# Two of 25 neighbour rows taken from SBUF by 0/1 products on TensorE, in a two-layer graph kernel

## The reference

```python
h = jnp.maximum(_layernorm(x, axis=-1), 0.0)
# layer 0, A = adj, S = 25
scores = jnp.where(A != 0, -jnp.arange(N), neg_inf)
vals, idx = jax.lax.top_k(scores, S)
feats = jax.vmap(lambda x, i: x[i])(h, idx)
feats = jnp.where((vals > neg_inf)[..., None], feats, neg_inf)
agg = feats.max(axis=2)
agg = jnp.where((degree <= S)[..., None], jnp.maximum(agg, 0.0), agg)
x = x + relu(concat([h, agg], -1) @ W0 + b0)
# layer 1
h = jnp.maximum(_layernorm(x, axis=-1), 0.0)
hidden = h @ W1.T
attn = leaky_relu(a1[:, :, None] + a2[:, None, :], 0.2)
attn = softmax(jnp.where(adj > 0, attn, attn - 1e12), -1)
x = x + attn @ hidden + bias
```

## Time and profile before

| what | us |
|---|---|
| median of 3 runs (4226.17 to 4229.52) | 4229.43 |
| the profiled execution, time | 4228.84 |
| the profiled execution, span | 4226.7 |
| GpSimd busy | 3064.6 (73%) |
| VectorE busy | 2596.7 (61%) |
| TensorE busy, products | 2441.5 (58%) |
| ScalarE busy | 1565.1 (37%) |
| mean granted clock of TensorE, share of full | 0.756 |

### The profile page before, as it was taken

One profiled execution on the slowest core, in us unless ns is written; L12 is line 12 of the kernel. 1 busy time (PEld: TensorE's weight loads), 2 busy tenths in 40 slices (PEclk: granted clock), 3 DMA queues, 4 the chain that ended last, 5 costly groups with the idle time before them and its releaser, 6 DMA issues. The chain is left out here.

```text
span 4226.7 us, 34008 instructions
## 1 busy us (share of the span) xinstructions
PE 2441.5 (58%) x8788; PEld 1510.5 (36%) x8788; DVE 2596.7 (61%) x6764; ACT 1565.1 (37%) x1748; POOL 3064.6 (73%) x3204
## 2 busy tenths in 40 slices
PE   1213345656555656565666565566556566656898
PEld 0111123433333434333334333343333343434565
DVE  5654566666666666666665676566676666566653
ACT  3112233334343434343434433334433334434354
POOL 4777777777777777777777777777777777777740
PEclk6555567777777878777878777777777777777899
DMA  7455568777777777777777777777777776777530
GB/s 288 150 189 174 189 180 232 195 219 214 230 211 228 204 223 216 217 220 219 212 215 216 216 228 211 228 207 209 218 228 215 224 207 213 214 211 223 179 106 35
DMA packets 477367, 867.56 MB, mean 205 GB/s; under 512 B 308298, under 2 KB 309204, under 8 KB 456660
## 3 DMA queue, kind: packets, MB, share of 16 engines
q0 software_dynamic: 153600, 419.64, 36.0%
q1 hardware_dynamic: 305140, 378.64, 28.8%
q10 hardware_dynamic: 18432, 67.12, 4.2%
HBM read 690.98 MB, written 119.54 MB: 192 GB/s over the span
## 5 line engine op out<-in xcount | busy, mean ns | idle before, releaser
L560 POOL DMA_INDIRECT near<-table_dram,idx x3200 | 3064.4, 958 | 1011.4 <-issue 961.1
L1406 PE MATMUL acc<-hid,wgt 128*128 128x257 f32 x4096 | 1051.5, 404 | 61.6 <-ACT wgt L642 54.4
L964 DVE TENSOR_TENSOR highest<-near,highest 128x512 f32<-128x512 f32 x1280 | 890.4, 696 | 43.8
L1406 PEld LDWEIGHTS acc<-hid,wgt 128*128 128x128 f32 x4096 | 817.0, 203 | 199.1 <-ACT wgt L642 72.2
L961 DVE TENSOR_TENSOR highest<-near 128x512 f32<-128x512 f32 x128 | 89.7, 701 | 814.8 <-DMA near<-table_dram,idx 813.4
L606 ACT ACTIVATE nm_t<-adj_i,big_c 128x2048 bf16<-128x2048 int32 x128 | 501.5, 3944 | 7.0 <-DMA adj_i<-in_adj_dram 3.4
L636 ACT ACTIVATE pen<-a_b,a_rise 128x512 f32<-128x512 f32 x432 | 296.5, 690 | 427.0 <-DMA nm_c<-nm_q 397.9
L1339 PE MATMUL bank<-w_sb,h_t 128*128 128x256 f32 x1024 | 348.0, 499 | 134.4 <-ACT h_t L739 134.4
L642 ACT ACTIVATE wgt<-pen,a_slope 128x512 f32<-128x512 f32 x448 | 304.2, 679 | 292.4 <-PE pen L1399 254.6
L739 ACT ACTIVATE h_t<-bank 128x512 f32<-128x512 f32 x128 | 76.0, 594 | 849.3 <-PE bank L1331 849.3
L898 DVE MAX8 top<-key 128x8 f32<-128x256 f32 (+1 forms) x1024 | 351.4, 384 | 5.6
(11 more groups left out here) (161 smaller groups left out, 2355.4 us busy)
## 6 DMA issues: line engine op xcount, KB each, us to landing
adj_i<-in_adj_dram SPq DMA_DIRECT2D x128, 1024.0 KB
nmask_dram<-nm_t ACTq DMA_DIRECT2D x128, 512.0 KB
nm_q<-nmask_dram SPq DMA_DIRECT2D x28, 2048.0 KB, 8.7
near<-table_dram,idx POOLq DMA_INDIRECT x3200
h_q<-table_dram SPq DMA_DIRECT2D x32, 512.0 KB, 3.9
x_q<-in_x_dram SPq DMA_DIRECT2D x32, 512.0 KB, 5.4
xmid_dram<-x_q SPq DMA_DIRECT2D x32, 512.0 KB, 4.3
o_q<-xmid_dram SPq DMA_DIRECT2D x32, 512.0 KB, 8.0
```

The source lines that it names most:

```text
L560: pool.indirect_dma_start(out=near[:, t % 2, k, :], out_offset=None, in_=table, in_offset=bass.IndirectOffsetOnAxis(ap=idx[:, t, k:k + 1], ...
L964: nc.vector.tensor_tensor(highest[:, :], pair(k), highest[:, :], ALU.max).then_inc(mx_step, 1)
L1406: mm = nc.tensor.matmul(acc[:, t, 0:C + 1], wgt_part(j)[:, t * P:(t + 1) * P], hid[:, bass.ds(batch * NJ + j, 1), 0:C + 1].rearrange("p a ...
```

## The change

In steps 0 to 29, tiles 1, 2 and 3, GpSimd gathers 23 rows instead of 25. The last two come from SBUF: a new tile `tab` holds all 2048 rows of the batch (`NJ` = 16 blocks of 128), loaded every fourth step in place of `h_q`. ScalarE widens the two index columns to 128x256, TensorE transposes them so that every partition holds all 128 indices, and ScalarE copies them back and clears `highest`. VectorE then compares, for each of the 16 blocks, the indices with that block's row numbers, into one of four buffers that lie over `bits` and `key2`; TensorE multiplies each 0/1 matrix, once for each of the two rows, with the block in `tab` and accumulates into `highest`. `maximum` starts from that. GpSimd's descriptor scratch is cut from its default to 8192 bytes a partition, and `near` holds two rows fewer. The cut diff:

```diff
+HOT_TILES = (1, 2, 3)
+HOT = 2
+HOT_BUFS = 4
...
-        near = sb("near", [P, 2, S, C], F32)
+        near = sb("near", [P, 2 * S - HOT, C], F32)
+        tab = sb("tab", [P, NJ, C], F32)
...
+        def is_hot(s, t):
+            return s < LAST - 1 and t in HOT_TILES
...
-                    sp.dma_start(h_q[:, :, :], table_quad(s % TRING)).then_inc(h_in, 16)
+                    if s % QB == 0:
+                        if s > 0:
+                            sp.wait_ge(table_out, 16 * s)
+                        for i in range(QB):
+                            sp.dma_start(tab[:, i * T:(i + 1) * T, :], table_quad((s + i) % TRING)).then_inc(h_in, 16)
...
-                    for k in range(S):
+                    for k in range(S - HOT if is_hot(s, t) else S):
...
+            def hot_row_copy(s, t):
+                n = hot_before(s, t)
+                act.wait_ge(hot_turned, n + 1)
+                nc.scalar.activation(agg[:, t % 2, :], highest[:, 0:HOT * P], ACT.Copy).then_inc(hot_rows, 1)
+                act.wait_ge(hot_rows, 2 * n + 1)
+                nc.scalar.activation(highest[:, :].rearrange("p (t m) -> p t m", t=T),
+                                     ident.unsqueeze(1).to_broadcast([P, T, P]), ACT.Copy, scale=0.0
+                                     ).then_inc(hot_rows, 1)
...
+            def hot_rows_made(s, t, groups=range(NJ // HOT_BUFS)):
+                n = hot_before(s, t)
+                for k in [HOT_BUFS * g + i for g in groups for i in range(HOT_BUFS)]:
+                    if k == 0:
+                        dve.wait_ge(hot_rows, 2 * n + 1)
+                    if k >= HOT_BUFS:
+                        dve.wait_ge(hot_used, NJ * n + k - HOT_BUFS + 1)
+                    col = C_HOT + s // QB % (TRING // QB) * NJ + k
+                    nc.vector.tensor_scalar(hot_bufs[k % HOT_BUFS], agg[:, t % 2, :], cst[:, col:col + 1], None, ALU.is_equal
+                                            ).then_inc(hot_made, 1)
...
+                if is_hot(s, t):
+                    dve.wait_ge(hot_used, NJ * (hot_before(s, t) + 1))
...
-                largest(a2_row, nm_q, junk, range(T), as_n)
+                for t in range(T):
+                    largest(a2_row, nm_q, junk, (t,), as_n)
+                    hot_rows_made(a + LAG, 1, (t,))
...
-                        index_rest(pair, between)
+                        dve.wait_ge(b2_free, b2.n + 1)
+                        hot_rows_made(s, 2, (0,))
+                        index_rest(pair, between, lambda r: hot_rows_made(s, 2, (r + 1,)), lambda: hot_rows_used(s, 2))
...
+                if "gather" in stages:
+                    dve.wait_ge(b2_free, b2.n + 1)
+                    hot_rows_made(s, 3)
                 gathered(3)
...
+            def hot_products(s, t):
+                n = hot_before(s, t)
+                pe.wait_ge(hot_rows, 2 * n + 2)
+                for k in range(NJ):
+                    pe.wait_ge(hot_made, NJ * n + k + 1)
+                    for i in range(HOT):
+                        mm = nc.tensor.matmul(highest[:, i * C:(i + 1) * C], hot_bufs[k % HOT_BUFS][:, i * P:(i + 1) * P],
+                                              tab[:, k, :], start=False, stop=(k == NJ - 1), skip_group_check=True)
+                    mm.then_inc(hot_used, 1)
...
                 gathered(0)
+                if "gather" in stages:
+                    hot_products(s, 1)
                 if "attend" in stages:
                     attend_setup(a)
...
                 gathered(1)
+                if "gather" in stages:
+                    hot_products(s, 2)
                 for c in range(8):
...
+                    if "gather" in stages and c == 3:
+                        hot_products(s, 3)
...
-    nc = _bacc.Bacc("TRN2", target_bir_lowering=False, num_devices=1)
+    nc = _bacc.Bacc("TRN2", target_bir_lowering=False, num_devices=1, dynamic_dma_scratch_size=8192)
```

More of the change, by code:

```diff
@@ L106, in shape_constants @@
         c[:, C_CODE + q] = BR * (q // QB % (TRING // QB)) + N + 0.25
+    for b in range(TRING // QB):
+        for k in range(NJ):
+            c[:, C_HOT + b * NJ + k] = BR * b + QR * (k // T) + T * np.arange(P) + k % T
     return c
@@ L328, in two_layers, with hot_before, landed @@
         block = ctx.enter_context(nc.Block())
+        def is_hot(s, t):
+            return s < LAST - 1 and t in HOT_TILES
+        def hot_before(s, t):
+            return len(HOT_TILES) * min(s, LAST - 1) + (sum(u < t for u in HOT_TILES) if s < LAST - 1 else 0)
+        def landed(s, t):
+            tiles = [(r, u) for r in range(s + 1) for u in (t % 2, t % 2 + 2) if (r, u) <= (s, t)]
+            return sum(S - HOT if is_hot(r, u) else S for r, u in tiles)
         def schedule(step):
@@ L557, in step @@
                     pool.nop(nofuse=True)
[L558 removed]
+                    for k in range(S - HOT if is_hot(s, t) else S):
                         attention(s, stages, t, k)
+                        spilt = t % 2 == 1 and k >= S - HOT
                         pool.indirect_dma_start(
[L561 removed]
+                            out=tab[:, k - (S - HOT), :] if spilt else near[:, t % 2 * S + k, :], out_offset=None, in_=table,
                             in_offset=bass.IndirectOffsetOnAxis(ap=idx[:, t, k:k + 1], axis=0),
@@ new lines, in hot_rows_used @@
+            def hot_rows_used(s, t):
+                if is_hot(s, t):
+                    dve.wait_ge(hot_used, NJ * (hot_before(s, t) + 1))
+            def maximum(s, t):
+                dve.wait_ge(near_in[t % 2], 16 * landed(s, t))
+                rows = near[:, t % 2 * S:, :]
+                pairs = [rows[:, k:k + 2, :].rearrange("p a c -> p (a c)") for k in range(0, S - HOT - 1, 2)]
+                if is_hot(s, t):
+                    dve.wait_ge(hot_used, NJ * (hot_before(s, t) + 1))
+                elif t % 2 == 0:
+                    pairs.append(rows[:, S - HOT:S, :].rearrange("p a c -> p (a c)"))
+                else:
+                    pairs.append(tab[:, 0:HOT, :].rearrange("p a c -> p (a c)"))
+                mx_n = Count()
+                if is_hot(s, t):
+                    nc.vector.tensor_tensor(highest[:, :], pairs[0], highest[:, :], ALU.max).then_inc(mx_step, 1)
+                    others = pairs[1:]
+                else:
+                    nc.vector.tensor_tensor(highest[:, :], pairs[0], pairs[1], ALU.max).then_inc(mx_step, 1)
+                    others = pairs[2:]
+                for pair in others:
```

79 lines of the change are left out of this document (56 added, 23 removed).

## The result

The changed kernel takes **4984.57 us** (median of 4 runs, 4972.56 to 5003.62) against 4227.8 us of the kernel before beside it. The ratio is 1.180, with a 95% interval of 1.176 to 1.183. The forecast was 5040 in a range of 4800 to 5180. The profiled execution took 4983.15 us, its span is 4981.3.

The account below looks back on a forecast made before the run. GpSimd bounds at 126.3 us a step, the other engines' chain close behind: 122.8 + 4.8 + 16.6 + 17.0 - 2.5 = 158.7, 32.4 more. 4228.8 + 26 x 32.4 - 30 = 5041, said 5040 us, range 4800 to 5180.

Parts of the forecast that it names:

- The second limit: TensorE, VectorE and ScalarE together: without GpSimd a step would take 122.8 us, 3.5 under GpSimd's pace of 126.3.
- the other engines' chain: Loop of TensorE, VectorE and ScalarE work through an attention step, maximum 0 to the next step's, put at 122.8 us.
- The block: A hot tile's 16 pairs of fp32 products on TensorE: 0.915 us a pair, 14.6 us, length set by TensorE.
- Block 1: Tile 1's products, behind layer 0 of tile 0: idle time covers 10 us, 4.8 us are new.
- Block 2: Tile 2's products, between layer 0 of tile 1 and chunk 0: adds 16.6 us, 1.5 for a lower clock.
- Block 3: Tile 3's products, between layer 0 of tile 2 and chunk 4: adds 17.0 us, 1.9 waiting for index words and a comparison.
- What comes back: TensorE's setup, packing product and chunk 0's first product find the higher clock: 2.5 us a step recovered.
- The mask wait: Wait of 10.90 us for a turned mask amid chunk 3: moves with the chunks, nothing given back.
- Steps 0 to 3: Steps without attention: GpSimd keeps setting the pace, its whole 7.5 us a step is saved, 30 us in all.
- It hides and is faster: Rival: all three blocks fall into TensorE's idle time, giving 4108 us, or 4004 at GpSimd's pace; chance 0.08.
- The low clock: Rival: gaps from comparisons bring TensorE's clock to 0.50, blocks take 29 us, over 6100 us in all; chance 0.03.
- Comparisons held by GpSimd: Rival: each VectorE comparison loses up to a gather's 0.95 us, takes 1.25, a block 20 us: 5450 us; chance 0.04.

Follow-up runs that it names:

- e_rows_dropped: The kernel before with 23 gathers in tiles 1 to 3 of steps 0 to 29 and nothing in place of the two rows: 4075.05 us, ratio 0.964.
- e_few_compared: The changed kernel with four comparisons in a block instead of 16, all products kept: 4975.47 us, ratio 1.176.
- e_tile1: The changed kernel with only tile 1 taking two rows from SBUF, `near` whole, descriptor scratch 6144 bytes: 4202.89 us, ratio 0.9945.
- e_tile2: The changed kernel with only tile 2 taking two rows from SBUF, `near` whole, descriptor scratch 6144 bytes: 4466.36 us, ratio 1.056.
- e_tile3: The changed kernel with only tile 3 taking two rows from SBUF, `near` whole, descriptor scratch 6144 bytes: 4525.13 us, ratio 1.070.
- e_one_product: The changed kernel with one product for each 0/1 matrix instead of two, all comparisons kept: 4559.6 us, ratio 1.078.
- e_all_gathers: The changed kernel with GpSimd gathering all 25 rows of every tile, TensorE still making the two rows: 5006.68 us, ratio 1.184.
- v_mixed: The changed kernel with all three tiles in steps 0 to 3 but only tile 1 in steps 4 to 29: 4215.79 us, ratio 0.9960.

## Why the prediction was right, and where its steps were off

**The second limit.** That the other engines' chain stands close behind GpSimd was the step that decided the sign. The forecast had it 3.5 us behind, at 122.8 of 126.3. `e_rows_dropped` puts it at 121.6 us or less, against 126.0 for a step of the kernel before: 4.4 us behind. Right, shown, and 0.9 us small.

**The block.** A pair was put at 0.915 us and measures 0.864. The reading was off, not the row: 0.457 us a call went up to the start of the next, different product, and the last section shows that this change costs 0.1 us by itself. That is 0.8 us a block, 2.4 a step, of the 3.9 that the forecast of 158.7 had over the measured 154.8. That TensorE and not the comparisons sets the length is shown by `e_few_compared`; a comparison takes 0.37 us instead of 0.3, which costs next to nothing, as said.

**Block 1** was to add 4.8 us, with the other 10 under idle time. Alone, in `e_tile1`, it leaves a step at 124.8 us, which is 1.2 under the kernel before and at most 3.2 over the chain of 121.6. Its place in an idle stretch is shown. In the step of the rows above maximum 1 starts 37.9 us into the step, because the layer product ahead of the block fell into a low clock (3.78 us); that is not typical, for in the mean of all steps this product took 2.6 us, and 2.9 before.

**Block 2** was to add 16.6, 1.5 of it for the low clock. The block itself had 1.00; the 1.5 did not arise there. In `e_tile2` a step takes 135.6 us, 9.6 over the kernel before and 13.9 over the chain.

**Block 3** was to add 17.0. Chunk 4 starts 2252.38 - 2233.97 = 18.4 us behind the residual of tile 2, and 2048.88 - 2046.51 = 2.4 before, so 16.0. By `e_tile3`, with 137.3 us a step, it is 11.3 over the kernel before and 15.7 over the chain. The three alone sum up to 32.8 us over the chain; together they made 154.8 - 121.6 = 33.2. So the prices nearly add, as the forecast took them to, and it had 35.9.

**What comes back** was put at 2.5 us: 1.5 for the packing product, 1.1 for chunk 0. The packing product takes 3.62 us in the rows above and 3.34 in the mean of all steps, 3.41 before, and not the 1.96 that block 1 ahead of it was to bring: that step failed, the clock in that stretch is 0.54. The row scores right behind the block did find the high clock, 1.10 us instead of 2.05. The first product of chunk 0 takes 1.90 us, as forecast, but before it was 2.35 in the mean of the steps and not the 2.96 of the one row that was read. That makes some 1.5 us. The mask wait was expected to move along whole; in the rows read, TensorE's idle time ahead of the penalty was 8.32 us and is 6.40 (the row at 2224.71).

**Steps 0 to 3 failed.** I took 30 us off because GpSimd has 7.5 us less to do there and nothing else seemed near. With three blocks these steps take 505.2 us and not 474. TensorE waits in them for maxima (11.46 and 9.07 us in step 2, ahead of the transposes of tiles 2 and 3), VectorE for blocks (the 2.84 us in the row at 355.40), one behind the other, and that loop is new. That it is made by the products is shown by `e_one_product`, where half of them bring the 30 us; the comparisons (`e_few_compared`, 504.2) and the gathers (`e_all_gathers`, 508.5) are not what sets it. I had looked for the loop with attention only. `v_mixed` then repeated the error and missed in the main for the same reason.

**Luck.** The errors partly cancel. The steps with attention were put 26 x (32.4 - 28.8) = 93 us too long; steps 0 to 3 were 31 too short, and the stretch from step 30 on, for which the forecast had no change, 5 too short. 5041 - 93 + 31 + 5 is the measured 4984. The mechanism was right for the 26 steps; that the sum came within 56 us owes something to the error in steps 0 to 3. With steps 0 to 3 put right it would have been 5072, further off and still inside the range.

**The rivals.** "It hides and is faster" is right for block 1 alone, and gives 24.5 us there; the kernel's other two blocks are past the few us that the chain could bear. The low clock was not in blocks 2 and 3. **Comparisons held by GpSimd** did occur, but at a size and in a number that don't count. Two rows of VectorE's timeline in block 3; both comparisons ran beside a gather:

```profile
2240.49 0.35 DVE L1025 TENSOR_SCALAR bits<-agg,cst 128x256 f32<-128x256 f32 x1 [0.48 <-PE highest L1436]
...
2245.67 0.59 DVE L1025 TENSOR_SCALAR key<-agg,cst 128x256 f32<-128x256 f32 x1 [0.51 <-PE highest L1436]
```

0.35 us is the common value. Of the 1440 comparisons of the trace 1098 overlapped a gather, and 137 of these took over 0.45 us, the longest 0.60; none of the 342 others took over 0.36. The mean of all is 0.37, where the rival had 1.25, and the gathers keep their median of 946 ns. `e_few_compared`, without three quarters of them, is 9 us faster, so what they lose to gathers costs hardly more. The Trainium skill, SBUF — State Buffer, section Who interferes with whom, has the later of the two engines blocked for a whole instruction when VectorE's uses both ports. No run here shows whether the comparisons did; if so, the delay that the trace shows, up to 0.25 us, is far from a whole gather of 0.95.

## What to carry to other kernels

An engine that has nothing but work may still be only one of two limits. Before work is moved away from it, follow the other engines' loop through a step, subtract the waits that really end on the bound engine, and see how far behind it stands: here 3.5 us by the sum and 4.4 by experiment, which capped a saving of 7.5 and turned some 41 us of new work on an engine with 42% idle time into 29 us a step. Moved work is free only in a stretch where its new engine, and everyone who waits for that engine, is idle; do the same sum for the steps at the edges of the program, whose loop is another one. And read an experiment by stretches of the program: a difference divided by the number of steps puts into one kind of step what arose in another.

## What the runs showed of the hardware that was not expected

The price of an fp32 product depends on what follows it. TensorE's timeline, two short windows of the changed kernel: the last instruction of block 2 and the first of chunk 0, then the last of that chunk's eight and the penalty behind it.

```profile
2198.13 0.38 PE L1436 MATMUL highest<-tab,key 128*128 128x256 f32 x1
2198.35 0.38 PE L1525 MATMUL acc<-hid,wgt 128*128 128x257 f32 x1
...
2199.86 0.38 PE L1525 MATMUL acc<-hid,wgt 128*128 128x257 f32 x1
2200.18 0.39 PE L1517 MATMUL pen<-m_r,ones_b 3*128 3x512 bf16 x1
```

At a granted clock of 1.00 the instructions of L1436, with 256 columns, start 0.216 us apart, those of L1525, with 257, 0.217 us, and the change from the one to the other costs nothing either. But the bf16 penalty with three rows starts 0.31 us behind the last fp32 instruction, 0.1 more. So eight instructions measured up to the penalty give 1.83 us and 0.457 a call, which the forecast took, and eight measured up to another fp32 product give 1.73 us and 0.432. What causes the 0.1 was not tried.

The granted clock fell in attention's setup, right behind a block of 15 us of dense products. It was 1.00 from 2156.50 to 2172.00, 0.63 from 2172.00 to 2174.70, and 0.50 from 2174.70 to 2178.40, in the packing product. Ahead of the fall lie waits of TensorE of 0.40, 0.73 and 1.49 us and small products between them; which of these brought it down stays open.
